# Accumulating transposes in place of products with the identity, in the scans and in the mixing of experts of a four-layer hybrid network

## What is computed

```
def step(h, inp):
    x_t, dt_t, B_t, C_t = inp
    A_bar = 1.0 + A[None] * dt_t[..., None]
    B_bar = B_t[:, None, :] * dt_t[..., None]
    h = A_bar * h + B_bar * x_t[..., None]
    y_t = jnp.sum(C_t[:, None, :] * h, axis=-1)
    return (h, y_t)
...
x = x + _L0_attn_a_ref(_layernorm(x, axis=-1), L0_attn_a_W_in, ...)
```

## Time and profile before

| | us |
|---|---|
| median of 3 runs | 3631.7 (3627.91 to 3641.34) |
| the profiled execution's own time | 3608.04 |
| its span | 3606.7 |
| PE busy | 3038.5 (84%) |
| DVE busy | 2381.2 (66%) |
| ACT busy | 2202.3 (61%) |
| POOL busy | 1394.7 (39%) |

### The profile page before, as it was taken

The page is one execution under the profiler, slowest core; times in us unless marked ns, Lnnn a source line. Parts: engine busy times, 40 slices in busy tenths (PEclk is TensorE's granted clock), DMA queues, the critical chain, the costliest instruction groups (busy, mean ns, idle before and its releaser), DMA issues. The chain is left out here.

```text
span 3606.7 us, 52771 instructions
## 1 busy us (share of the span) xinstructions
PE 3038.5 (84%) x18500; PEld 1822.3 (51%) x18500; DVE 2381.2 (66%) x6084; ACT 2202.3 (61%) x4827; POOL 1394.7 (39%) x1308
## 2 busy tenths in 40 slices
PE   3678887999889999889999887878788787789987
PEld 0244556657545555444555434546545476554344
DVE  2778774675777776667768889965444444655764
ACT  2456554534466777667767766947656566466874
POOL 1445554444345554224646554643220222100320
PEclk9889998999999999999999999989988999789997
DMA  6343343113200010220101123543532254321420
GB/s 228 97 128 111 105 112 109 57 44 100 68 14 1 1 32 8 76 52 15 51 1 33 33 81 100 166 130 103 135 82 61 61 178 112 99 46 31 92 52 10
DMA packets 216897, 271.96 MB, mean 75 GB/s; under 512 B 39544, under 2 KB 154936, under 8 KB 214584
## 3 DMA queue, kind: packets, MB, share of 16 engines
q1 hardware_dynamic: 192312, 191.11, 18.7%
q0 software_dynamic: 24320, 77.47, 7.2%
HBM read 217.02 MB, written 54.00 MB: 75 GB/s over the span
## 5 line engine op out<-in xcount | busy, mean ns | idle before, releaser
L371 ACT ACTIVATE scratch<-psum 128x512 f32<-128x512 f32 (+6 forms) x1780 | 828.0, 497 | 808.2 <-PE psum L327 578.7
L327 PE MATMUL psum<-scratch 128*128 128x128 f32 (+19 forms) x8016 | 942.9, 324 | 110.2 <-ACT scratch L371 51.0
L463 POOL TENSOR_TENSOR scratch<-scratch 128x512 f32<-128x512 f32 (+3 forms) x536 | 614.7, 1162 | 697.0 <-DVE scratch L424 216.0
L327 PEld LDWEIGHTS psum<-scratch 128*32 128x32 f32 (+9 forms) x8016 | 601.2, 148 | 476.9 <-issue 224.4
L327 PE MATMUL psum<-scratch,w_constants 128*128 128x512 f32 (+2 forms) x848 | 453.5, 635 | 131.8 <-DVE scratch L393 110.2
L371 ACT ACTIVATE scratch<-scratch 128x512 f32<-128x512 f32 (+8 forms) x856 | 395.8, 469 | 246.5 <-DVE scratch L393 167.1
L363 ACT ACT_TABLE_LOAD x357 | 458.0, 1283 | 23.5 <-DVE scratch L393 9.1
L393 DVE TENSOR_TENSOR scratch<-psum,scratch 128x512 f32<-128x512 f32 (+2 forms) x696 | 376.2, 551 | 115.0 <-ACT scratch L371 83.3
L343 PE MATMUL psum<-w_constants,scratch 128*128 128x128 f32 (+2 forms) x1880 | 316.3, 289 | 61.0 <-ACT scratch L371 22.4
L407 DVE TENSOR_TENSOR_SCAN psum<-psum,scratch 128x512 f32<-128x512 f32 x256 | 309.3, 1222 | 77.1 <-ACT psum L371 63.5
L371 ACT ACTIVATE psum<-scratch 128x255 f32<-128x255 f32 (+1 forms) x528 | 221.4, 456 | 193.2 <-DVE scratch L393 188.2
(11 more groups left out here) (108 smaller groups left out, 4016.0 us busy)
## 6 DMA issues: line engine op xcount, KB each, us to landing
scratch<-b_and_c_out SPq DMA_DIRECT2D x256, 256.0 KB
slots_out<-scratch SPq DMA_DIRECT2D x112, 128.0 KB
q_stack<-scratch SPq DMA_DIRECT2D x72, 192.0 KB, 2.4
scratch<-q_out SPq DMA_DIRECT2D x96, 96.0 KB
scratch<-slots_in SPq DMA_DIRECT2D x16, 512.0 KB
q_out<-scratch SPq DMA_DIRECT2D x40, 192.0 KB, 3.1
scratch<-slots_in SPq DMA_DIRECT2D x16, 448.0 KB
scratch<-q_stack SPq DMA_DIRECT2D x24, 288.0 KB
```

The lines of the kernel that those rows point to most:

```text
L327: return self.engine.matmul(out, lhsT, rhs, start=start, stop=stop, **kw)
L371: return self.engine.activation(out, src, function, **kw)
L463: return self.engine.tensor_tensor(out, a, b, op)
```

## The change

Each sum over states is made of four float32 transposes of 128 x 128, which add into PSUM, in place of one product with the identity of 512 columns. Bank `a` then holds the sum with tokens on the partitions. After the sixteenth state ACT copies it into a scratch buffer (`y_token`, the buffer `h[2]`), and PE turns it back with four ordinary transposes into bank `a` again. The skip term waits for that turn in place of the last product. In `ExpertMix`, four products become four accumulating transposes. The weights of the gated linear attention start at column 2048 of their buffer (2 x SPARE) and not at 2034; their load and its size are the same.

```
+    def add_turned(self, out, src, ident, start, stop):
+
+        self.spend(out, src, 109, 1)
+        return self.engine.matmul(out, src, ident, start=start, stop=stop, is_transpose=True)
...
+        self.y_token = v2(self.h[2].rearrange("p a b -> p (a b)"), P)
...
             for n in range(N):
                 e.wait_ge(*(yield self["cmul", bt, n]))
-                e.matmul(self.a, self.c["ident"], self.h[n % 3].rearrange("p a b -> p (a b)"), start=(n == 0),
-                         stop=(n == N - 1)).then_inc(*self.post("acc", bt, n))
+                for i in range(TILES):
+                    chunk, d = divmod(i, D)
+                    last = e.add_turned(self.a[:, i * P:(i + 1) * P], self.h[n % 3][:, d, chunk * P:(chunk + 1) * P], self.c["ident"],
+                                        start=(n == 0 and i == 0), stop=(n == N - 1 and i == TILES - 1))
+                last.then_inc(*self.post("acc", bt, n))
...
             last.then_inc(*self.post("z_in", bt))
+            e.wait_ge(*(yield self["token", "y", bt]))
+            for i in range(TILES):
+                chunk, d = divmod(i, D)
+                last = e.transpose(self.A2[:, d, chunk * P:(chunk + 1) * P], self.y_token[:, i, :], self.c["ident"])
+            last.then_inc(*self.post("turn", "y", bt))
...
             e.wait_ge(*(yield self["acc", bt, N - 1]))
+            e.activation(self.y_token, v2(self.a, P), ACT.Copy).then_inc(*self.post("token", "y", bt))
             e.wait_ge(*(yield self["z_in", bt], ACT.Silu))
...
-            e.wait_ge(*(yield self["acc", bt, N - 1]))
+            e.wait_ge(*(yield self["turn", "y", bt]))
...
-            last = e.matmul(self.a[:, t * P:(t + 1) * P], self.by_token[:, 0, t, :], self.c["ident"], start=False, stop=(t == TILES - 1))
+            last = e.add_turned(self.a[:, t * P:(t + 1) * P], self.by_token[:, 0, t, :], self.c["ident"], start=False, stop=(t == TILES - 1))
...
-FROM = {"L1_attn": 3 * SPARE, "L2_scan": 4 * SPARE}
+FROM = {"L1_gla": 2 * SPARE, "L1_attn": 3 * SPARE, "L2_scan": 4 * SPARE}
```

## The result

| | before | changed |
|---|---|---|
| median | 3632.8 us (4 runs, 3627.9 to 3641.3) | 3790.3 us (4 runs, 3778.7 to 3795.3) |
| ratio, with its 95% interval | | 1.0426 (1.0395 to 1.0457) |
| span of the profiled execution | 3606.7 | 3794.0 |

What follows compares the result with a forecast made beforehand. DVE and one state's chain were taken to hold the scans, PE the stretch between them. -26 + 8 + 10 + 20 = +12 us on the median of 3631.7 gave 3643 us, with an 8-in-10 range of 3590 to 3690.

Steps and rivals of the forecast that it cites:

- The gain of -26 us: Waits for PE shorten by 0.65 us each: 15 us from DVE's 23, 11 from ACT's in the second scan.
- The bound of 0: Waits for PE: no gain at all if PE's queue was never their cause; the other bound was -92 us.
- the 118 of the prediction: PE time given back by the exchange: 115 us over 256 states and 3 us in the mixing.
- case 4: In the scans: the clock falls from 0.93 to 0.75, costing 37 us on the path, 3680 us; 6%.
- The end of each scan, +8 us: Copy and turn delay what follows by 0.8 us at each of 16 scan ends; bounds 0 and 21.
- Table loads, +10 us: On ACT: 19 more loads take 24 us, of which 40% lies on the path; bounds 0 and 24.
- The end of the program, +20 us: Last stream's tail: 48 us longer, less 28 us for an earlier end of the first stream; bounds 0 and +48.
- +48: Program's end: 153 DVE instructions after the first stream's end, at 1.2 us, take 184 us, 48 more than 136.
- Case 2: At the program's end: the last stream alone decides, nothing offsets the 48 us tail; +40, 3672 us; 31%.
- a gain of 28 us: Program's end: the first stream ends earlier, with 25 more DVE instructions and some 21 us of PE work left.
- The 147 more clock-keeping products: On PE where it would be idle: put at nothing; up to 50 us of PE, 5 on the path, if work waits.
- 108 us at 84%: Bound of the gain: PE's useful work saved times its busy share, if every stretch is bound by PE; -92 us.

Runs made afterwards that it cites:

- the pair on one chip: Against the kernel before: the changed kernel's order with products, 1.0431, and the old order with transposes, copy and turn, 1.0036.
- `scan_only`: Against the kernel before: accumulating transposes in the scans alone, mixing as before, planner's own order; 0.9976, and 1.0059 when run again on another chip.
- `mix_only`: Against the kernel before: accumulating transposes only in the mixing of experts, scans keep their products, planner's own order; 1.0037.

## Why the prediction was wrong, step by step

**The gain of -26 us was not there.** It rested on waits for PE that would get shorter by 0.65 us apiece. The waits of the kernel with the old order and the new operations, first scan, then second:

```profile
DVE scratch L408 <- PE psum L335: 31.9, 21, 9.0
```

```profile
ACT scratch L386 <- PE psum L335: 54.7, 51, 3.2
ACT scratch L386 <- PE psum L356: 17.7, 7, 9.5
```

DVE's waits went from 33.3 us in 23 to 31.9 in 21, that is from 1.45 to 1.52 us each. ACT's went from 62.4 in 57 to 54.7 in 51, 1.09 to 1.07 each. The 17.7 us of waits for the accumulating transposes (L356) come with the new copy, which waits for the last of them. The same waits in the kernel without copy and turn:

```profile
DVE scratch L409 <- PE psum L336: 32.0, 23, 8.5
```

```profile
ACT scratch L387 <- PE psum L336: 53.2, 51, 2.6
ACT scratch L387 <- PE psum L357: 2.6, 3, 1.4
```

That is 1.39 and 1.04 us each: a wait that PE ends got shorter by 0.05 us or so, if at all (the replay with products has 1.61 and 1.10), and not by 0.65. That most of them last as long as the product's own chain of work, and not as long as a queue, fits this, but I only argue it. The bound of 0 which the prediction kept was the right value, to within some 8 us: without copy and turn the kernel gave 1.0004 (0.9985 to 1.0023).

**PE gave back less than counted, perhaps in part by the clock.** The price was right: four accumulating transposes in a row took 0.60 to 0.66 us in the changed kernel's timeline of PE (280 to 300 us; start, us, count), and eight took 1.04, so four in a queue add 0.44:

```profile
284.89 0.60 PE L348 MATMUL psum<-w_constants,scratch 128*128 128x128 f32 x4
...
288.17 1.04 PE L348 MATMUL psum<-w_constants,scratch 128*128 128x128 f32 x8
```

In one order, busy time fell by 29 and 35 us in the two scans where some 51 (391 less 340) had been forecast for the first. Over the whole span it fell by 54 us (3038.5 to 2984.4) and, without copy and turn, by 73; 108 had been forecast. The groups show where the rest went. First before (what fell away stands in these two, with other products):

```profile
L327 PE MATMUL psum<-scratch,w_constants 128*128 128x512 f32 x752 | 434.2, 673 | 130.2 <-DVE scratch L393 109.8 <-ACT scratch L371 15.3 <-issue 2.3
L327 PE MATMUL psum<-w_constants,scratch 128*128 128x128 f32 x64 | 11.1, 326 | 0.0
```

Then in the old order with the new operations (what is left of the first, and what came):

```profile
L335 PE MATMUL psum<-scratch,w_constants 128*128 128x512 f32 x240 | 136.5, 653 | 18.2 <-ACT scratch L386 14.8 <-DVE scratch L427 2.3 <-issue 0.6
L356 PE MATMUL psum<-w_constants,scratch 128*128 128x128 f32 x1056 | 197.1, 324 | 152.9 <-DVE scratch L408 149.8 <-issue 2.5
L335 PE MATMUL psum<-bf_masks 128*128 128x512 bf16 x532 | 188.1, 444 | 10.8 <-issue 4.7 <-ACT scratch L386 2.1 <-DVE scratch L435 1.6
```

The exchange itself gave back 112 us, near the 118 of the prediction, and other work took half of it away: the same 532 clock-keeping products take 188.1 us where they took 179.5, the ordinary transposes 18 us more, with 64 of them added. The clock fell in the scans with the operations, 0.91 to 0.84 and 0.95 to 0.89, which fits products that last longer; how much of the rest is the clock's was not measured. So the mechanism of case 4 is real, with a fall of 0.06 to 0.07 where it assumed 0.18, but its cost did not show: in all the accumulation came to 1.0004, which fits a PE that does not hold the scans. The lowest stretch is 100 to 200 us, with PE busy 55 of 100 at 0.66 (before, 64 at 0.86). The Trainium skill, "TensorE: Matmul & The Clock Gate", Part 4 (PE-mode transpose), says that a transpose doesn't count as PE-busy in the same way and the full clock doesn't engage for it. The traces agree in sparse stretches alone, where the clock fell by 0.06 to 0.07 over a scan; in 5 us with 24 transposes and other work it stood at 1.00. And in the scans PE also had less to do (362 us for 391), so no run shows that it was the kind of the work, and not its amount, that the clock fell with.

**The end of each scan, +8 us, is not contradicted.** Copy and turn come to 1.0036 less 1.0004, some 12 us, with an uncertainty of about 9 from the two intervals, and they are of two chips. The scan's group kept its 1222 ns and its idle time of about 30 us (34.1, and 29.1 in the old order), as forecast.

**Table loads, +10 us.** 19 more came, and ACT's busy time rose by 38 us. What they cost by themselves was not measured, and the list above speaks against reading it off their number: the kernels with 321 and 280 of them lose 2.7% and 3.2%, and one with 358, as before, 2.8%.

**The end of the program, +20 us, is the term that was mis-sized, and the one that was thought complete and wasn't.** It was bounded by +48, from 153 DVE instructions at 1.2 us. Measured, the distance between the last stream and the mean grew by 105 us, two thirds of the loss between the medians. The time from the first end to the last, for which the +48 stood, grew by 127. It is 260 us where 184 had been worked out, or 1.7 us for each of the 153 instructions: two streams ended 21 us apart, and in the last 129 us the clock stood at 0.54 and PE, on which one stream's chain waits, was busy for 59% of the time. Case 2, "the last stream alone decides", was the nearest, but gave 3672. And 25 DVE instructions more that are left at the first stream's end were set against the loss as a gain of 28 us. The first stream did not end earlier by that: it ended 61 us later. (The 30 us in that step were worked out from 21 us of PE work at 2000 us in the span of 3607, which makes 38.)

**The other failed step is one that the prediction did not write down as one.** It costed the new order at three places (scans' ends, tables, program's end) and held that elsewhere "DVE's, POOL's and SP's work is the same", so the rest cost nothing. But the streams' mean end is 83 us later in the profiles (nearer to 50 between the medians, and 44 in the pair on one chip), a lag of all four streams that builds up from the linear attention on, a block in which no operation changed. The same work in another order takes another time, by 0.8% to 4.3% in eight of the ten orders that ran here besides that of before (of the other two, `scan_only` gave -0.2% and +0.6% on two chips and `mix_only` +0.4%, each with its operations). A rival "the order by itself costs some per cent, with no term of the change in it" was missing. It would have needed no theory: the diff plans 4 x 109 = 436 ns where 256 products were planned at 860.

The 147 more clock-keeping products were put at nothing too. No run prices them alone; `mix_only`, with 69 more than the kernel before, is at 1.0037.

**Signs and sums.** Most of the signs that were to show the prediction right came true in a kernel that is 4.3% slower: DVE's scan group kept its 1222 ns, four transposes took 0.60 to 0.66 us, the table loads took 24 us more of ACT, the first two stores came over 150 us ahead of the end, and the clock there was low. They test the terms that were written down, and none tests the pace of the streams elsewhere. Two bounds were summed wrongly, without weight for the result: 108 us at 84% make 91 and not 92, and case 2 with table loads and scans' ends at their bounds is 3699 and not 3690.

**Still open** is what in an order makes the lag. The table loads, the end, the streams' distance and the number of clock-keeping products were each at or under the value of before in a kernel that stayed slow, so none of them is the whole cause. The traces show only that every engine's idle time grows together.

## What to carry to other kernels

- Where a planner sets the order from costs, a changed cost is a second change, and it can outweigh the first. Replay one recorded order with both sets of operations (a replay of the unchanged kernel gave 0.9992), and the two effects stand apart.
- Nudge a planned cost by 1 ns before an effect of a few per cent is believed. Here that gave 1.008 and 1.035. The order of before was as good as any of the eleven that were measured, so a new draw was likelier to lose than to gain; why that order was so good is not on record.
- Work taken from the engine that is busiest over the whole program can be worth nothing in a stretch that this engine does not hold. Here PE did 73 us less in the kernel without copy and turn, and its time was 1.0004 of before.

## What the runs showed of the hardware

- Float32 transposes of 128 x 128 that accumulate in PSUM take 0.11 us each in a queue (four more in a row, 0.44 us), the same as the ordinary ones in the earlier trace rows.
- The same order with transposes in place of products has a lower granted clock in the scans: 0.84 against 0.91, and 0.89 against 0.95.
- The ratio of two kernels can differ between chips (or groups of runs; each chip had one) by more than their intervals: `scan_only` gave 0.9976 (0.9959 to 0.9993) on one and 1.0059 (1.0035 to 1.0082) on another, while the kernel before itself ran in 3530.9 and 3631.9 us.
